# Row maxima put into a 97th row of the score contraction, with the exact scores a pair step further behind

## What is computed

```python
x = layernorm(x + splat_attention(x))          # k=0: 256 keys, features of 16 per head
x = layernorm(x + cross_attention(x, ctx))     # k=1: 120 keys, head dim 16
x = layernorm(x + best_expert_of_8(x))
x = layernorm(x + causal_attention(x))         # k=2: 256 keys, head dim 16
x = layernorm(x + mha_block(x, x, causal mask after the softmax) ... + mha_block(x, ctx))
                                               # k=3: 256 keys, k=4: 120 keys, head dim 32
x = layernorm(x + four_experts_of_16(x))
```

## Time and profile before

| | |
|---|---|
| median of 3 runs | 3753.8 us (3750.38 to 3755.05) |
| profiled execution: its own time | 3753.18 us |
| profiled execution: span, first to last instruction | 3751.0 us |
| mean granted TensorE clock in it | 0.924 |
| busy share of the span | PE 83%, PEld 65%, DVE 72%, ACT 56%, POOL 26% |

### The profile page before, as it was taken

One profiled execution on the slowest core, in us unless ns is written; L12 is line 12 of the kernel. 1 busy time (PEld: TensorE's weight loads), 2 busy tenths in 40 slices (PEclk: granted clock), 3 DMA queues, 4 the chain that ended last, 5 costly groups with the idle time before them and its releaser, 6 DMA issues. The chain is left out here.

```text
span 3751.0 us, 89546 instructions
## 1 busy us (share of the span) xinstructions
PE 3123.4 (83%) x34864; PEld 2456.7 (65%) x34864; DVE 2699.4 (72%) x6135; ACT 2105.0 (56%) x4254; POOL 978.4 (26%) x1793
## 2 busy tenths in 40 slices
PE   1989888888888978888988888798988897988886
PEld 1767666766676757766766666676756676766664
DVE  6868676777676767767777667687777677768765
ACT  4745665555556554564565555646655556466542
POOL 1312341122223321231133222212343113124310
PEclk9999899999899989989998988999999999999987
DMA  6211211112112121121121111212121112122110
GB/s 199 70 55 56 79 61 53 45 45 67 55 54 72 48 62 41 50 67 55 48 72 56 54 53 38 70 45 71 60 67 60 39 41 68 48 62 71 60 37 6
DMA packets 362006, 221.49 MB, mean 59 GB/s; under 512 B 102497, under 2 KB 333298, under 8 KB 361586
## 3 DMA queue, kind: packets, MB, share of 16 engines
q1 hardware_dynamic: 361586, 215.76, 19.0%
HBM read 122.23 MB, written 93.32 MB: 57 GB/s over the span
## 5 line engine op out<-in xcount | busy, mean ns | idle before, releaser
L1158 ACT ACTIVATE p<-bank,p_log 128x512 f32<-128x512 f32 (+2 forms) x1280 | 748.3, 585 | 1122.3 <-PE bank L850 1019.3
L1712 POOL TENSOR_TENSOR prob<-p,prob 120x256 f16<-120x256 f32 (+2 forms) x512 | 451.7, 882 | 1650.9 <-ACT prob L1159 1650.5
L1159 ACT ACTIVATE prob<-bank,p_log 128x512 f16<-128x512 f32 (+2 forms) x1280 | 749.3, 585 | 0.0
L1417 DVE TENSOR_REDUCE negm<-bank 128x2 f16<-128x512 f32 (+1 forms) x1280 | 674.8, 568 | 98.9 <-PE bank L813 89.2
L1347 DVE TENSOR_TENSOR prob<-p,prob 128x512 f16<-128x512 f32 (+2 forms) x768 | 485.6, 641 | 92.6 <-ACT prob L1159 88.5
L720 PE MATMUL bank<-w_exp,ident_h 128*128 128x512 f16 x1280 | 418.9, 411 | 101.7 <-DMA k_ring<-k_heads 85.8
L829 PE MATMUL bank<-q_ring,k_ring 80*128 80x256 f16 (+4 forms) x2048 | 445.1, 284 | 40.8 <-ACT raw L1105 14.4
L850 PE MATMUL bank<-ident_h,negm 128*128 128x256 f16 (+2 forms) x2560 | 440.7, 259 | 0.0
L1721 POOL TENSOR_SCALAR_AFFINE_SELECT probm<-prob 128x128 f16<-128x128 f16 x1024 | 326.7, 357 | 308.9 <-DVE prob L1347 308.9
L813 PE MATMUL bank<-k_ring,q_ring 80*128 80x256 f16 (+4 forms) x2560 | 368.5, 259 | 34.8 <-DVE negm L1417 34.2
L813 PEld LDWEIGHTS bank<-k_ring,q_ring 80*128 80x128 f16 (+1 forms) x2560 | 236.5, 104 | 234.2 <-issue 51.5
(11 more groups left out here) (299 smaller groups left out, 6190.1 us busy)
## 6 DMA issues: line engine op xcount, KB each, us to landing
q_ring<-q_heads SPq DMA_DIRECT2D x768, 40.0 KB, 2.2
q_heads<-q_made SPq DMA_DIRECT2D x96, 256.0 KB, 2.4
k_heads<-k_made SPq DMA_DIRECT2D x96, 256.0 KB, 2.3
q_ring<-q_heads SPq DMA_DIRECT2D x512, 48.0 KB, 2.2
k_ring<-k_heads SPq DMA_DIRECT2D x512, 40.0 KB, 2.2
q_heads<-q_made SPq DMA_DIRECT2D x144, 128.0 KB, 1.8
k_heads<-k_made SPq DMA_DIRECT2D x144, 128.0 KB, 1.8
k_ring<-k_heads SPq DMA_DIRECT2D x256, 48.0 KB, 2.2
```

The source lines that it names most:

```text
L1158: act(p32[0:n, g % PBUF32, 0:cols], ps[0:n, 0:cols], ACT.Exp, bias=p_log[0:n, :], scale=a.scale)
L1159: act(prob[0:n, 0, g % PBUF, 0:cols], ps[0:n, 0:cols], ACT.Exp, bias=p_log[0:n, :], scale=a.scale).then_inc(a_done, one(a_done))
L1417: v.tensor_reduce(negm[:, h * NT:(h + 1) * NT], ring_v[bank_of(e, v_full)][:, :].rearrange("p (t n) -> p t n", t=NT)[:, :, 0:ATTNS[k].keys ...
L1712: g.tensor_tensor(prob[0:n, 1, m % PBUF, 0:cols], p32[0:n, m % PBUF32, 0:cols], prob[0:n, 0, m % PBUF, 0:cols], ALU.subtract).then_inc(pp_ ...
```

## The change

EXACT_LAG goes from 2 to 4 heads, PV_LAG from 4 to 6, and a third lag, TURN_LAG = 2, is new. In step n, TensorE now does the row scores of pair n, then for pair n-1 four matmuls of 128 columns (`maxima_to_row`: `negm` spread over the weights against the identity) into a whole bank of `ring_a`, then the exact scores of pair n-2, then the weighted values of pair n-3. ACT copies one partition of the new bank, 512 elements (the maxima of both heads), into partition 96 of the pair's slot in `q_ring` (`row_of_maxima`); partition 96 of `k_ring` is set to one at the start. The exact scores contract over 97 rows, and the L850 matmuls are gone. All heads use 96 stacked rows, so head dim 16 gets a third plane of zeros (12 instead of 8 DMAs store them in the setup), and the fills of head dim 16 bring 96 instead of 80 rows. The fill of pair m still waits for the exact scores of pair m-4, which now come in step m-2 instead of m-3.

The tables move: EARLY and the last part by four turns, LATE for k=0, 2 and 4 by up to five, LATE for k=1 and 3 not, LATE_SOON by two to four.

```diff
 STREAM_NORM, STREAM_GATES, STREAM_HEADS, STREAM_ROWS = 0, 0, 0, 2
-EXACT_LAG = 2
-PV_LAG = 4
+TURN_LAG = 2
+EXACT_LAG = 4
+PV_LAG = 6
...
-    3: (("oT", 9), ("out", 13), ("norm2", 14), ("norm4", 19)),
...
+    3: (("oT", 13), ("out", 17), ("norm2", 18), ("norm4", 23)),
...
-    0: (("xT", 2), ("q_raw", 4), ("q", 7), ("k_raw", 10), ("k", 15), ("v", 18)),
+    0: (("xT", 2), ("q_raw", 4), ("q", 7), ("k_raw", 14), ("k", 17), ("v", 20)),
...
-LATE_SOON = {1: (("xT", 18), ("q", 21), ("k", 23), ("v", 28)), 3: (("xT", 22), ("q", 24), ("k", 25), ("v", 28))}
+LATE_SOON = {1: (("xT", 22), ("q", 24), ("k", 26), ("v", 30)), 3: (("xT", 26), ("q", 28), ("k", 29), ("v", 32))}
...
-        q_ring, k_ring = (sb(f"{what}_ring", [96, SLOTS, PAIR, TOK], F16) for what in "qk")
-        heads16 = {what: nc.dram_tensor(f"{what}_heads16", (2, 5, P, 2 * TOK), F16).ap() for what in "qk"}
-        heads32 = {what: nc.dram_tensor(f"{what}_heads32", (2, 3, P, 4 * TOK), F16).ap() for what in "qk"}
+        q_ring, k_ring = (sb(f"{what}_ring", [STACKED + 1, SLOTS, PAIR, TOK], F16) for what in "qk")
+        heads16 = {what: nc.dram_tensor(f"{what}_heads16", (2, STACKED // 16, P, 2 * TOK), F16).ap() for what in "qk"}
+        heads32 = {what: nc.dram_tensor(f"{what}_heads32", (2, STACKED // 32, P, 4 * TOK), F16).ap() for what in "qk"}
...
-                        for plane in (3, 4):
+                        for plane in (3, 4, 5):
...
+                step(g.memset(k_ring[STACKED:STACKED + 1, :, :, :], 1.0))
...
                         if g == pair[0]:
                             e.wait_ge(ring_full[g // PAIR % SLOTS], slot_filled(g // PAIR))
-                        q, kk = operands(g)
+                        q, kk = operands(g, STACKED)
...
+                def maxima_to_row(pair):
+
+                    ps = slot("a", "row", pair[0] // PAIR)
+                    e.wait_ge(*moved("max", pair[1]))
+                    for at, g in enumerate(pair):
+                        for i in range(NT):
+                            column = ORDER[g][2] * NT + i
+                            c = (at * NT + i) * P
+                            last = mm(ps[:, c:c + P], negm[:, column:column + 1].broadcast_to([P, P]), ident_h[:, :],
+                                      start=(at, i) == (0, 0), stop=(at, i) == (PAIR - 1, NT - 1))
+                    last.then_inc(a_full, one(a_full))
+
                 def exact_scores(pair):
 
                     for g in pair:
-                        a, h = ATTNS[ORDER[g][0]], ORDER[g][2]
-                        q, kk = operands(g)
+                        a = ATTNS[ORDER[g][0]]
+                        q, kk = operands(g, STACKED + 1)
                         ps = slot("a", "p", g)
+                        if g == pair[0]:
+                            e.wait_ge(*moved("row", g // PAIR))
                         for j, (k0, n) in enumerate(a.key_tiles):
                             i0 = j * P if a.causal else 0
-                            mm(ps[0:n, j * TOK:j * TOK + TOK - i0], kk[:, k0:k0 + n], q[:, i0:TOK],
-                               start=j == 0, stop=False)
-                        e.wait_ge(*moved("max", g))
-                        n = a.key_tiles[0][1]
-                        rows = ps[0:n, :].rearrange("p (j c) -> p j c", j=NT)
+                            last = mm(ps[0:n, j * TOK:j * TOK + TOK - i0], kk[:, k0:k0 + n], q[:, i0:TOK],
+                                      start=j == 0, stop=not a.causal and k0 + n == a.keys)
                         if a.causal:
-                            blocks = rows[:, :, 0:P]
-                            mm(blocks, ident_h[:, :], mask_k[:, :].rearrange("p (a n) -> p a n", a=1
-                                                                             ).broadcast_to([P, NT, P]),
-                               start=False, stop=False)
-                        for i in range(NT):
-                            if a.causal:
-                                o = ps[0:n, 0:P] if i == 0 else ps[0:n, P:TOK + P].rearrange("p (j c) -> p j c", j=NT)
-                                times = 1 + i
-                            else:
-                                o, times = rows[:, 0:len(a.key_tiles), i * P:i * P + P], len(a.key_tiles)
-                            moving = ident_h[:, :]
-                            if a.causal and i == 0:
-                                pass
-                            else:
-                                moving = moving.rearrange("p (a n) -> p a n", a=1).broadcast_to([P, times, P])
-                            last = mm(o, negm[:, h * NT + i:h * NT + i + 1].broadcast_to([P, n]), moving,
-                                      start=False, stop=i == NT - 1)
+                            blocks = ps[:, :].rearrange("p (j c) -> p j c", j=NT)[:, :, 0:P]
+                            last = mm(blocks, ident_h[:, :], mask_k[:, :].rearrange("p (a n) -> p a n", a=1
+                                                                                    ).broadcast_to([P, NT, P]),
+                                      start=False, stop=True)
                         last.then_inc(a_full, one(a_full))
                     freed["ring", pair[0] // PAIR] = a_full, sent(a_full)
...
+                    if 0 <= n - TURN_LAG < len(ORDER):
+                        maxima_to_row((n - TURN_LAG, n - TURN_LAG + 1))
                     if 0 <= n - EXACT_LAG < len(ORDER):
                         exact_scores((n - EXACT_LAG, n - EXACT_LAG + 1))
...
+                def row_of_maxima(m):
+
+                    e.wait_ge(a_full, upcoming(e, a_full))
+                    ps = ring_a[bank_of(e, a_full)]
+                    act(q_ring[STACKED:STACKED + 1, m % SLOTS, :, :].rearrange("o h n -> o (h n)"),
+                        ps[STACKED:STACKED + 1, :], ACT.Copy).then_inc(a_done, one(a_done))
...
+                    if 0 <= n - TURN_LAG < len(ORDER):
+                        row_of_maxima((n - TURN_LAG) // PAIR)
                     for g in (n - EXACT_LAG, n - EXACT_LAG + 1):
                         if 0 <= g < len(ORDER):
                             exponentials(g)
...
-                        begin = max((m - SLOTS + 1) * TURNS + 2, PLACE[(k, b), "k"] + 0.5)
+                        begin = max((m - SLOTS + EXACT_LAG // PAIR) * TURNS + 2, PLACE[(k, b), "k"] + 0.5)
```

More of the change, by code:

```diff
@@ L52 @@
 SLOTS = 4
+STACKED = 96
 PLANES = {"q": (0, 1, 0), "k": (0, 0, 1)}
@@ L509, in _ @@
                 e.wait_ge(w_ready[1], w_count[1])
-                e.wait_ge(zeros_stored, 16 * 8)
+                e.wait_ge(zeros_stored, 16 * 12)
             @block.gpsimd
@@ L793, in values, with operands @@
                             token_major(ws, col, 512, src, n_in, [tile], "a", *what, by="dve")
-                def operands(g):
+                def operands(g, rows):
                     a, h = ATTNS[ORDER[g][0]], ORDER[g][2]
                     slot_of, at = g // PAIR % SLOTS, h % PAIR
-                    return q_ring[0:a.stacked, slot_of, at, :], k_ring[0:a.stacked, slot_of, at, 0:a.keys]
+                    return q_ring[0:rows, slot_of, at, :], k_ring[0:rows, slot_of, at, 0:a.keys]
                 def row_scores(pair):
```

13 lines of the change are left out of this document (6 added, 7 removed), and 4 rows, old and new, of the table LATE.

## The result

The changed kernel takes 4,218.8 us (median of 4 runs, 4,210.8 to 4,226.1) against 3,752.6 (4 runs, 3,750.4 to 3,755.1): 1.124 times as long, 95% interval 1.122 to 1.127. Forecast were 3,830 us and a range of 3,725 to 3,935. The sign was right, the size was far off: +466 us where the sum gave +78.

What follows compares the result with a forecast made beforehand. No engine was full; PE led, waiting about a quarter of the span. Terms -42 + 38 + 41 + 52 + 20 + 6 = +115, less 37, gave +78 us: 3,830 us, range 3,725 to 3,935.

Steps and rivals of the forecast that it cites:

- the term for the ring slots: Ring fills and ACT: shorter time from slot release to next use lengthens short steps; +38 us with the copy, ends 0 and 113.
- Columns, -42 us: PE: replacing the L850 matmuls saves 70 us of columns at full clock, of which 60% is taken.
- the forecast's 60%: PE: share of saved column time counted as saved run time, since PE issues in three quarters of the span.
- PE's columns decide: Rival: PE is last in most steps, all 70 us count, stalls mostly vanish; faster, 3,700 to 3,745 us; chance 0.19.
- Banks, +52 and +20: ring_a: a third bank a step makes exact scores and row matmuls wait, +52 us; 358 stages wait for the row's bank, +20.
- The copy, inside the +38: ACT: 640 copies at 0.58 us, 371 us more work, delaying exponentials by some 0.3 us, hidden by the next step.
- ACT becomes the bound: Rival: the copy counts in full in short steps, 113 us instead of 38, nothing taken off; 3,945 us; chance 0.14.
- LATE_SOON, +41: PE at phase starts: less cover before first row scores; 29 us after LATE_SOON[3], 12 after LATE_SOON[1]; ends 20 and 55.
- A third taken off, -37: Discount on the 110 us of slots, banks and row waits, as stalls partly fall into the same steps.
- Short steps: The 195 of 640 steps under 3.5 us, 2.7 on average; forecast to last 2.95 us or more.
- Short steps stay at 2.7 us: Sign against the forecast: short steps not lengthening from their 2.7 us would show it wrong.
- The Trainium skill: PE: at its 81 ns per 128-column matmul the saving would be 37 us, the total 20 us higher; the row was used.

Runs made afterwards that it cites:

- e5: Changed kernel, four slots, with most stores of q and k, the fetches and the result sends four turns later in SP's list: 4,073.2 us.
- e1: Changed kernel with five instead of four slots in the q and k rings, so fills may again start three steps ahead: 4,031.0 us.
- e2: Kernel before with three instead of four ring slots, giving its fills the change's lead of two steps, nothing else changed: 4,011.9 us.
- e16: Kernel before with one stream matmul a step instead of two, 136 us less columns: 3,756.3 us.
- e15: Changed kernel with five slots and three stream matmuls a step instead of two, 136 us more columns: 4,050.8 us.
- e8: Kernel before plus the row matmuls, row not read, with ACT copying 8 elements instead of 512: 3,836.7 us.
- e9: Kernel before plus unread row matmuls of 16 columns instead of 128, with ACT copying 8 elements: 3,847.6 us.
- e17: Kernel before with the change's lags, tables and fill places, five slots, the unread row matmuls and a copy of 8 elements: 3,931.0 us.
- e7: Kernel before with the change's lags, tables and fill places and five slots, maxima still added by the L850 matmuls: 3,839.1 us.
- e3: Kernel before, four slots, with the change's lags, tables and later fills, maxima still added by the L850 matmuls, no row or copy: 4,081.3 us.
- e4: Kernel before plus the row matmuls and ACT's full copy, row not read; lags, places and slots as before: 3,900.7 us.
- e10: Kernel before with the change's lags, tables and fill places, five slots, the unread row matmuls and the full copy: 4,013.8 us.

## Why the prediction was wrong, step by step

The failed step is the term for the ring slots, "I take **+38 us** for slots and ACT together". It let each fill begin at its slot's release, counted 4.2 us to landing, and looked only at the 195 short steps. What it priced exists: fill waits with nothing between release and fill have 30 us, before 5. But the description of the kernel before says that a fill also waits for the stores ahead of it in SP's list, and the prediction had no term for it. With a step less of lead, 69 row scores waited for fills behind stores and fetches that themselves wait for DVE and ACT (157 us, before 18). e5 shows it, with 150 us of the 466; the slots' lead as a whole is 190 (e1), and 257 where nothing else is changed (e2). The top of that term, 113, was too low as well.

- **Columns, -42 us: next to nothing.** 136 us of columns less are worth +2 us in the kernel before (e16), 136 more cost 20 in the changed one (e15), where the forecast's 60% would be 82. The rival "PE's columns decide" falls with it. I had counted PE's issue time as if it ran against the end; PE waits somewhere in 395 of the 640 steps before and in 515 in the changed kernel, and what it does not spend on columns it waits for banks, maxima and fills.
- **Banks, +52 and +20: 80 to 94** (e8, e9, e17), the short copy included. The mechanism fits the waits, and 72 was a fair size. The idle before L845 and L831 was 187 us where 90 were forecast; not all of it costs time.
- **The copy, inside the +38: 66 to 83.** Duration and ACT's total were right. It was put at almost nothing because the next step hides it; it does not. The rival "ACT becomes the bound" came nearest, with 3,945 us, and was still 274 short: it had 113 us for the copy, and no rival had a price for the queue of the fills.
- **LATE_SOON, +41:** the six waits after LATE_SOON[3] grew by 27 where 29 were forecast, the other six not at all where 12 were. Lags and places together cost 82 to 95 (e7), of which 50 are fill waits.
- **A third taken off, -37: the overlap exists, but it was not the whole of it.** The row method costs 54 us less where the lead is short (140 against 194), and on the later places it costs 48 more than the row beside the kernel before (194 against 146). Lead 257 (e2), lags and places on top of it 70 (e3 less e2), row 146 (e4) are 472 us for 466 because these two nearly cancel, and that is luck.
- **Sum of the chain with five slots:** 82 (e7) + 94 (e17) + 83 (e10) + 17 (e1) = 276; with the lead, +190 = 466. Each term is the difference of two runs that follow each other, so the sum must come out; it gives the sizes and proves nothing.
- **Short steps:** they did not grow to 2.95 us, they became rare. 108 steps are under 3.5 us (2.74 on average), before 195; the tenth percentile went from 2.47 to 2.97 us. "Short steps stay at 2.7 us" was among the prediction's own signs of being wrong.
- **The Trainium skill** ("TensorE: Matmul & The Clock Gate", section "Back-to-back issue gap") has 81 ns for a sustained matmul of 128 columns. The changed kernel's timeline, and the row of its line (ns min/median/max):

```profile
2508.89 0.39 PE L831 MATMUL bank<-ident_h,negm 128*128 128x128 f16 x4
```

```profile
L831 PE MATMUL bank<-ident_h,negm x2560: 216/219/314, 95.8 to 4115.3; 128*128 128x128 f16 x197
```

  Four take 0.39 us where one takes 0.219: 57 ns from start to start. The row disagrees again, and the choice did not matter, since columns count for next to nothing here.

How much of the loss is the lower clock is not taken apart. By the mean granted clock, the lower level held for some 570 us before, 1,000 in the changed kernel and 900 in e2. From start-to-start distances of the same matmuls at either level I estimate that PE lost some 200 us to it before, 340 in the changed kernel and 320 in e2. So about 120 of e2's 257 us may come with the lower clock that follows the gaps. No run held the clock and the gaps apart.

What stays open: the 45 us of lags and places that are no fill waits, how the 80 to 94 us divide between the bank and the short copy, and what a fourth bank is worth beyond 56 us.

## What to carry to other kernels

When a buffer's lead gets shorter, look at the queue that refills it, not only at the loop of release and refill: whatever waits ahead of the refill in an in-order list is now on the path. Here moving it back in the list gave 150 us and needed no memory, where another slot gave 190. Before counting saved matmul columns as time, take some away that nobody needs (here one stream matmul a step): if the time stays, columns are no term to count on. And two stalls that add up in one comparison may overlap in another: compare the same part with and without the others (here the row method, 140 and 194 us) before a discount is put in or left out.

## What the hardware showed that I had not expected

- ACT's copy of one partition by 512 elements takes 589 ns, by 8 elements 170 ns (16 partitions by 512: 579): the length decides, 0.83 ns an element on top of some 163.
- More columns on TensorE, a higher granted clock: 0.901 to 0.921 (e1 to e15), and 0.924 to 0.895 with fewer (e16). Between e9 and e8, with 79 us more columns, 0.919 and 0.937. No run held the one and varied the other, so that the clock pays for the columns is an inference.
